# Projection of the node features by rounded high and low parts of weight and features, the weight arriving in two halves

## The chip, the cores and the metric

The kernel runs on one core of a Trainium2 chip. The metric is the device time of one execution in microseconds. The engines are named as the profile names them: PE (TensorE, PEld its weight loads), DVE (VectorE), ACT (ScalarE), POOL (GpSimd) and SP (SyncE, which issues most of the DMA transfers).

## The reference, cut to what matters

Four layers follow one another on 512 node vectors of 768 numbers. The change lies in the first step of the first layer, the projection of the normalised features:

```python
edge_index = jnp.stack([src, dst])                     # 8192 edges, 512 nodes
x = x + _L0_gnn_ref(_layernorm(x), ...)                # three rounds of message passing, attention
x = x + _L0_ffn_ref(_layernorm(x)[None], ...)[0]       # 8 experts, 2 chosen for each node
x = x + _L1_gnn_ref(_layernorm(x), ...)                # two graph attention layers
x = x + _L1_ffn_ref(_layernorm(x)[None], ...)[0]       # 4 experts, 1 chosen

def _L0_gnn_ref(node_features, ...):
    nodes = node_features @ Wn.T + bn                  # 512x768 by 768x768: the step that changes
    edge_proj = edge_features @ We.T + be
    for l in range(3):
        msgs = nodes[src] + nodes[dst] + edge_proj
        agg = jax.ops.segment_sum(msgs, dst, num_segments=n)
        ...
```

## The kernel before, in words

Everything stays in on-chip memory between the layers, and every engine has one program written out by hand in a fixed order; semaphores alone hold them together. There is no planner. `N` is 512 nodes, `NT` = 4 tiles of 128 nodes, `D` = 768, `DC` = 6 blocks of 128 features. Weights arrive in four slots (`slot[0]` to `slot[3]`, 128 x 4608 each), and `part_slot[s]` is the same memory seen as fp32r, the type in which PE takes a rounded fp32 number in one go. PE results go to eight PSUM banks: four (`act_ps`) that ACT empties, four (`dve_ps`) that DVE empties.

The start of the program runs like this.

- SP issues all first loads (L517 to L537): the features `xres` in four tiles, small constants, the weight `wn` into slot 0, indices, two groups of edge features, `we` into slot 1, and the two halves of the first round's weight into slots 2 and 3.
- DVE normalises the features tile by tile (`normalise`, L1762): three tiles together, then the fourth.
- PE turns the normalised tiles around (`turn_features`, L691; 24 transposes, L703) into six banks, one for each block of 128 features.
- ACT and DVE copy three banks each into `xn_t` (L1402, L1811).
- PE multiplies (L740): for each of six output blocks `c`, six matmuls over `k`, each with a 128x128 block of the weight as the kept operand and 128x512 of `xn_t` as the moving one, all in fp32. ACT and DVE take every second result into `nodes_t` with the bias (L1410, L1824).
- PE turns `nodes_t` back into rows (L713), ACT and DVE copy it to `nodes`. ACT has rounded two groups of edge features meanwhile (`ea_hi`, L1406), and DVE forms their remainders (`ea_lo`, L1837).
- Then comes the loop over 64 groups of 128 edges (L758 and L1881), the three rounds, attention, the experts and so on.

Most other products of this kernel are already made in another way, by the helper `mm_parts` (L720): an operand is split into its rounded value (`hi`) and what is left (`lo`), both fp32r, and three matmuls stand for one: hi by hi, hi by lo, lo by hi. In every such place ACT makes the high part by a copy and DVE the low part by a subtraction. The first graph attention layer does this for its features just as the change does it here (L1696 for `xn2_hi`, L2446 for `xn2_lo`).

Of the kernel before, what the change touches and what calls it, by code (L numbers as in the profile page):

```python
# [28 lines left out]
P = 128  # L29
# [7 lines left out]
N = 512  # L37
# [92 lines left out]
def build(nc, x, src, dst, edge, cols, rows, ident_d, iota_d, tri_d, wn, we, w1, w2, wqkv, wo, wg0, e0w1,  # L130
          e0w2, e0b2, gw1, gw2, wg1, e1w1, e1w2, e1b2, xs0, ys0, xs1, ys1, out):
    ctx = ExitStack()
    with ctx:
# [13 lines left out]
        def sem(name):  # L147
            return ctx.enter_context(nc.semaphore(name))
# [53 lines left out]
        def over(name, shape, at, dt=F32):  # L202
            return place(name, shape, dt, area + at)
# [5 lines left out]
        xn_t = over("xn_t", [P, DC, N], 6144)  # L209
# [108 lines left out]
        class Run:  # L318
            def __init__(self, layer, ne, hidden, picks, up, down, scattered, results, b1, b2, up_slots, down_slots, sel_banks, pick_banks):
# [11 lines left out]
                self.filled = sem(f"filled{layer}")  # L331
                self.scattered_in = sem(f"scattered{layer}")
                self.gathered = [sem(f"gathered{layer}_{t}") for t in range(NT)]
                self.sel_set = sem(f"sel_set{layer}")
                self.plan_set = sem(f"plan_set{layer}")
                self.b2_in = sem(f"b2_in{layer}")
                self.last_set = sem(f"last_set{layer}")

        sig0, sig1 = Signals("a"), Signals("b")
# [6 lines left out]
        in_par = sem("in_par")  # L346
        in_ends = sem("in_ends")
# [11 lines left out]
        act_step = sem("act_step")  # L359
# [135 lines left out]
        def _(sp):  # L495
# [27 lines left out]
            load(0, sview(0, DC, D), kview(wn))  # L523
# [59 lines left out]
            def stream_items(run):  # L583

                sp.wait_ge(run.plan_set, 1)
# [40 lines left out]
            def narrow_items(run):  # L626


                sp.wait_ge(run.plan_set, 1)
# [48 lines left out]
        def _(pe):  # L678
# [348 lines left out]
            def rank_tokens(run):  # L1027

                spend(act_ps[3], (14, 6)[run.layer])
                pe.wait_ge(run.sel_set, 1)  # L1030
# [37 lines left out]
            def stream_items(run):  # L1068
# [69 lines left out]
                pe.wait_ge(run.plan_set, 1)  # L1138
# [16 lines left out]
                pe.wait_ge(run.last_set, 1)  # L1155
# [15 lines left out]
            def narrow_items(run):  # L1171
# [52 lines left out]
                pe.wait_ge(run.plan_set, 1)  # L1224
# [13 lines left out]
                pe.wait_ge(run.last_set, 1)  # L1238
# [153 lines left out]
        def _(act):  # L1392
# [199 lines left out]
            def stream_items(run):  # L1592
# [36 lines left out]
                act.wait_ge(run.plan_set, 1)  # L1629
# [9 lines left out]
            def narrow_items(run):  # L1639
# [19 lines left out]
                act.wait_ge(run.plan_set, 1)  # L1659
# [84 lines left out]
        def _(dve):  # L1744
# [458 lines left out]
            def make_plan(run, choices):  # L2203
# [48 lines left out]
                dve.wait_ge(run.plan_set, 1)  # L2252
# [358 lines left out]
            dve.wait_ge(run1.sel_set, 1)  # L2611
# [3 lines left out]
            for t in range(NT):  # L2615
                dve.wait_ge(run1.gathered[t], 16)
# [9 lines left out]
        def _(pool):  # L2626
# [130 lines left out]
```

## Time and profile before

| what | value |
|---|---|
| median of 3 runs | 1350.22 us (1344.23, 1350.22, 1350.96) |
| profiled execution, its own time | 1348.07 us |
| its span, first to last instruction | 1346.5 us |
| PE busy | 95% of the span |
| DVE, ACT, POOL busy | 68%, 43%, 9% |
| mean granted TensorE clock | 0.991 of full speed |

The span is what all rows are counted in; the device time of the same execution lies 1.57 us above it. PE is busy nearly all of the time, but in a fixed order over stages with different limits, so the shares say little of one stage. A PE row named MATMUL shows a modelled end, which overlaps the start of the next one: the pace of a row of matmuls is read from start to start, not from their durations. An fp32 matmul appears as two records (12 for six matmuls).

### The profile page before, as it was taken

To read this page: it belongs to the slowest core of one execution; us is meant where nothing else is said; L and a number is where in the kernel's file an instruction comes from. 1 tells how busy PE (TensorE), PEld (TensorE's weight loads), DVE (VectorE), ACT (ScalarE), POOL (GpSimd) and SP (SyncE) were. 2 spreads that over 40 slices of the span, in tenths; PEclk is the share of its full clock that TensorE was granted. 3 is DMA by queue.
4 is the path that set the end of the run, shared out by engine and by line. 5 is a ranking of instruction groups with operands and counts; after the bars stand their busy time and mean duration, and the time that the engine had idled before them with its cause. 6 is when DMAs were issued, how large, how long until landed. Compare 5 with 4: busy or idle time off the path is not lost. (4 is left out here: it accounts for less than half of the span.)

```text
span 1346.5 us, 19432 instructions
## 1 busy us (share of the span) xinstructions
PE 1280.1 (95%) x7053; PEld 1099.5 (82%) x7054; DVE 911.3 (68%) x1828; ACT 582.8 (43%) x1013; POOL 127.0 (9%) x123
## 2 busy tenths in 40 slices
PE   5999999999999999999999999999999898899997
PEld 2577659969969997666999999999998778796864
DVE  4477683473473465555859999999998778836623
ACT  2011051351350343334418888888986227502110
POOL 0000010000000000003320000000002018600101
PEclk9999999999999999999999999999999998999899
DMA  9321091410410620003158999999998310007134
GB/s 340 136 94 63 9 359 55 153 71 1 153 71 1 235 95 0 1 24 141 67 209 295 356 382 389 390 386 392 389 382 281 137 28 1 1 1 293 47 105 164
DMA packets 80687, 225.46 MB, mean 167 GB/s; under 512 B 5168, under 2 KB 17008, under 8 KB 80496
## 3 DMA queue, kind: packets, MB, share of 16 engines
q1 hardware_dynamic: 72720, 187.64, 37.7%
q0 software_dynamic: 7904, 36.97, 7.6%
q8 instruction: 42, 0.69, 0.2%
q14 instruction: 21, 0.17, 0.0%
HBM read 197.85 MB, written 26.74 MB: 167 GB/s over the span
## 5 line engine op out<-in xcount | busy, mean ns | idle before, releaser
L2116 DVE TENSOR_TENSOR part_slot<-slot,item_hi 128x768 fp32r<-128x768 f32 x150 | 133.5, 958 | 0.2
L1557 ACT ACTIVATE item_hi<-slot 128x768 fp32r<-128x768 f32 x156 | 118.0, 833 | 23.9 <-DMA slot<-in_e0w 19.6
L2125 DVE TENSOR_TENSOR part_slot<-slot,item_hi 128x768 fp32r<-128x768 f32 x132 | 116.6, 954 | 1.7 <-ACT item_hi L1565 1.3
L1565 ACT ACTIVATE item_hi<-slot 128x768 fp32r<-128x768 f32 x132 | 99.1, 831 | 14.6 <-DMA slot<-in_e0w 14.6
L722 PE MATMUL dve_ps<-item_hi,x_hi 128*128 128x384 f32 x288 | 99.3, 345 | 0.5 <-DVE x_lo L2305 0.3
L722 PE MATMUL act_ps<-item_hi,hid_hi 128*128 128x384 f32 x288 | 98.4, 342 | 0.3 <-DVE hid_lo L2317 0.3
L724 PE MATMUL dve_ps<-item_hi,x_lo 128*128 128x384 f32 x288 | 97.2, 338 | 0.0
L723 PE MATMUL act_ps<-part_slot,hid_hi 128*128 128x384 f32 x288 | 96.8, 336 | 0.0
L724 PE MATMUL act_ps<-item_hi,hid_lo 128*128 128x384 f32 x288 | 96.1, 334 | 0.0
L723 PE MATMUL dve_ps<-part_slot,x_hi 128*128 128x384 f32 x288 | 95.6, 332 | 0.0
L1448 ACT ACTIVATE h_t<-act_ps,par 128x256 f32<-128x256 f32 x36 | 21.1, 585 | 121.5 <-PE act_ps L833 121.5
L729 PE MATMUL act_ps<-ones 128*128 128x128 f32 x470 | 62.7, 294 | 8.3 <-DVE gp_t L2520 6.3
L729 PEld LDWEIGHTS act_ps<-ones 128*128 128x128 f32 x470 | 60.3, 208 | 10.9 <-DVE gp_t L2520 6.7
L722 PE MATMUL dve_ps<-h_hi,w_hi 128*128 128x256 f32 x216 | 61.3, 284 | 0.0
L723 PE MATMUL dve_ps<-h_lo,w_hi 128*128 128x256 f32 x216 | 60.7, 281 | 0.0
L724 PE MATMUL dve_ps<-h_hi,part_slot 128*128 128x256 f32 x216 | 60.5, 280 | 0.0
L1967 DVE TENSOR_TENSOR h<-dve_ps,brow 128x384 f32<-128x384 f32 x24 | 13.4, 558 | 63.0 <-PE dve_ps L724 63.0
L722 PEld LDWEIGHTS dve_ps<-item_hi,x_hi 128*128 128x128 f32 x288 | 54.1, 188 | 0.9 <-DVE x_lo L2305 0.5
L722 PEld LDWEIGHTS act_ps<-item_hi,hid_hi 128*128 128x128 f32 x288 | 54.0, 187 | 0.5 <-issue 0.5
L723 PEld LDWEIGHTS dve_ps<-part_slot,x_hi 128*128 128x128 f32 x288 | 54.2, 188 | 0.0
L723 PEld LDWEIGHTS act_ps<-part_slot,hid_hi 128*128 128x128 f32 x288 | 54.2, 188 | 0.0
L724 PEld LDWEIGHTS act_ps<-item_hi,hid_lo 128*128 128x128 f32 x288 | 54.0, 188 | 0.0
(407 smaller groups left out, 3268.9 us busy)
## 6 DMA issues: line engine op xcount, KB each, us to landing
slot<-in_e0w SPq DMA_DIRECT2D x48, 2304.0 KB, 10.4
slot<-in_w SPq DMA_DIRECT2D x9, 2304.0 KB, 9.4
experts<-in_e1w SPq DMA_DIRECT2D x8, 1152.0 KB, 15.3
ea_raw<-in_edge SPq DMA_DIRECT2D x8, 1024.0 KB, 5.5
slot<-in_wqkv SPq DMA_DIRECT2D x3, 2304.0 KB, 14.8
xs<-zrow POOLq DMA_DIRECT2D x2, 3072.0 KB, 15.7
item_x<-xs SPq DMA_DIRECT2D x16, 384.0 KB, 9.6
ys<-item_y POOLq DMA_DIRECT2D x16, 384.0 KB, 6.7
```

Source lines behind the costliest of these rows:

```text
L722: mm(to, kept[0], moved[0], start=start, stop=False)
L723: mm(to, kept[0], moved[1], start=False, stop=False)
L724: return mm(to, kept[1], moved[0], start=False, stop=stop)
L729: mm(bank[:, 0:P], ones[:, :], ones[:, :], start=True, stop=True)
L1448: go(h_t[:, c, ps], turned, ACT.Relu, bias=col("ln_b", at), scale=col("ln_g", at))
L1557: go(item_hi[j][k][:, :], slot[s][:, k * D:(k + 1) * D], ACT.Copy).then_inc(up_high[j], 1)
L1565: go(item_hi[j][k][:, :], slot[s][:, k * D:(k + 1) * D], ACT.Copy).then_inc(down_high[j], 1)
L1967: vv.tensor_tensor(part, bank[:, 0:HALF], brow[:, 0, half * HALF:(half + 1) * HALF], ALU.add).then_inc(sig.dve_freed, 1)
L2116: vv.tensor_tensor(part_slot[s][:, ks], slot[s][:, ks], item_hi[j][k][:, :].bitcast(F32), ALU.subtract).then_inc(up_low[j], 1)
L2125: vv.tensor_tensor(part_slot[s][:, ks], slot[s][:, ks], item_hi[j][k][:, :].bitcast(F32), ALU.subtract).then_inc(down_low[j], 1)
```

## The change

Five things change in the code.

1. `xn_t` goes. In its place stand `xn_hi` and `xn_lo`, both fp32r; `xn_lo` lies where `xres` was, which is dead by then.
2. The weight is split as well: `wn_hi` in six pieces (four in the free part of slot 1, two over `mask`), the low part in place in slot 0, through `part_slot[0]`.
3. ACT makes the six pieces of `wn_hi` and all six of `xn_hi`; DVE makes six low pieces of the weight and all six of `xn_lo`, in the order written.
4. PE uses `mm_parts` for each of the 36 products. For the first output block it waits piece by piece.
5. SP loads `wn` by two transfers (rows 0 to 383 and 384 to 767), the first with a semaphore of its own.

Beside that, some semaphores that the two expert layers had one each of (`filled`, `gathered`, `sel_set`, `plan_set`, `last_set`) are now shared, and each wait on them counts on from the first layer's value.

```diff
-        xn_t = over("xn_t", [P, DC, N], 6144)
+        xn_hi = over("xn_hi", [P, DC, N], 6144, F32R)
+        xn_lo = place("xn_lo", [P, DC, N], F32R, xres_at)
+        wn_hi = [place(f"wn_hi{k}", [P, D], F32R, at) for k, at in
+                 enumerate([4608 + 1536 + D * k for k in range(4)] + [cpt_at, cpt_at + D])]
...
-            load(0, sview(0, DC, D), kview(wn))
+            sp.dma_start(sview(0, DC, D)[:, 0:3, :], kview(wn[0:3 * P, :])).then_inc(in_wn, 16)
+            load(0, sview(0, DC, D)[:, 3:DC, :], kview(wn[3 * P:DC * P, :]))
...
-            pe.wait_ge(slot_in[0], 16)
-            pe.wait_ge(sig.act_freed, ACT0["wn"])
-            pe.wait_ge(sig.dve_freed, DVE0["wn"])
-            wn_s = kslot(0, D)
             for c in range(DC):
-                bank = act_bank(c // 2, ACT0["wn"]) if c % 2 == 0 else dve_bank(c // 2, DVE0["wn"])
+                if c == 0:
+                    bank = act_ps[0]
+                else:
+                    bank = act_bank(c // 2, ACT0["wn"]) if c % 2 == 0 else dve_bank(c // 2, DVE0["wn"])
+                fs = slice(c * P, (c + 1) * P)
                 for k in range(DC):
-                    last = mm(bank[:, :], wn_s[:, k, c * P:(c + 1) * P], xn_t[:, k, :], start=(k == 0), stop=(k == DC - 1))
+                    if c == 0:
+                        pe.wait_ge(wn_low, k + 1)
+                        if k % 2 == 0:
+                            pe.wait_ge(sig.act_freed, ACT0["xt0"] + k // 2 + 1)
+                        else:
+                            pe.wait_ge(sig.dve_freed, DVE0["xt0"] + k // 2 + 1)
+                    last = mm_parts(bank[:, :], (wn_hi[k][:, fs], kslot(0, D, True)[:, k, fs]), (xn_hi[:, k, :], xn_lo[:, k, :]),
+                                    start=(k == 0), stop=(k == DC - 1))
                 last.then_inc(sig.to_act if c % 2 == 0 else sig.to_dve, 1)
...
-            for c in range(0, DC, 2):
-                bank = bank_of(c // 2, ACT0["xt0"])
-                go(xn_t[:, c, :], bank[:, :], ACT.Copy).then_inc(sig.act_freed, 1)
+            for k in range(DC):
+                act.wait_ge(*((in_wn, 16) if k < 3 else (slot_in[0], 16)))
+                go(wn_hi[k][:, :], slot[0][:, k * D:(k + 1) * D], ACT.Copy).then_inc(wn_high, 1)
+            for c in range(DC):
+                if c % 2 == 0:
+                    act.wait_ge(sig.to_act, ACT0["xt0"] + c // 2 + 1)
+                else:
+                    act.wait_ge(sig.to_dve, DVE0["xt0"] + c // 2 + 1)
+                go(xn_hi[:, c, :], (act_ps if c % 2 == 0 else dve_ps)[c // 2][:, :], ACT.Copy).then_inc(xn_high, 1)
...
-            for c in range(1, DC, 2):
-                bank = bank_of(c // 2, DVE0["xt0"])
-                vv.tensor_copy(xn_t[:, c, :], bank[:, :]).then_inc(sig.dve_freed, 1)
+
+            def low_node_weights(k):
+                ks = slice(k * D, (k + 1) * D)
+                dve.wait_ge(wn_high, k + 1)
+                vv.tensor_tensor(part_slot[0][:, ks], slot[0][:, ks], wn_hi[k][:, :].bitcast(F32), ALU.subtract).then_inc(wn_low, 1)
+
+            for k in range(4):
+                low_node_weights(k)
+            for c in range(DC):
+                bank, freed = ((act_ps[c // 2], sig.act_freed), (dve_ps[c // 2], sig.dve_freed))[c % 2]
+                dve.wait_ge(xn_high, c + 1)
+                vv.tensor_tensor(xn_lo[:, c, :], bank[:, :], xn_hi[:, c, :].bitcast(F32), ALU.subtract).then_inc(freed, 1)
+                if c in (1, 3):
+                    low_node_weights(4 + c // 2)
...
-                pool.wait_ge(run.filled, 64)
+                pool.wait_ge(run.filled, 128)
                 pool.wait_ge(normed, normed_by)
-                pool.wait_ge(run.plan_set, 1)
+                pool.wait_ge(run.plan_set, run.layer + 1)
```

On DVE, this stood between the end of the normalisation (`xn`) and the first result of the projection (`nodes_t`) before:

```order
35 L1798 TENSOR_SCALAR xn<-xres,mv,rstd 128x768
36 L1811 COPY xn_t<-dve_ps 128x512 x3
37 L1813 CAST ends<-ends_i 128x128
38 L1815 TENSOR_SCALAR src_w<-ends 128x64
39 L1817 SCALAR_TENSOR_TENSOR src_at<-src_w,ends 128x64
40 L1819 TENSOR_SCALAR src_w<-src_w 128x64
41 L1820 TENSOR_SCALAR zero<-iota 128x512
42 L1824 TENSOR_SCALAR nodes_t<-dve_ps,par 128x512 x3
```

And now (`slot_49` is slot 0, `part_slot_54` the same memory as fp32r, `wn_hi_108` to `wn_hi_113` the six pieces):

```order
35 L1820 TENSOR_SCALAR xn<-xres,mv,rstd 128x768
36 L1835 TENSOR_TENSOR part_slot_54<-slot_49,wn_hi_108 128x768
37 L1835 TENSOR_TENSOR part_slot_54<-slot_49,wn_hi_109 128x768
38 L1835 TENSOR_TENSOR part_slot_54<-slot_49,wn_hi_110 128x768
39 L1835 TENSOR_TENSOR part_slot_54<-slot_49,wn_hi_111 128x768
40 L1842 TENSOR_TENSOR xn_lo<-act_ps,xn_hi 128x512
41 L1842 TENSOR_TENSOR xn_lo<-dve_ps,xn_hi 128x512
42 L1835 TENSOR_TENSOR part_slot_54<-slot_49,wn_hi_112 128x768
43 L1842 TENSOR_TENSOR xn_lo<-act_ps,xn_hi 128x512
44 L1842 TENSOR_TENSOR xn_lo<-dve_ps,xn_hi 128x512
45 L1835 TENSOR_TENSOR part_slot_54<-slot_49,wn_hi_113 128x768
46 L1842 TENSOR_TENSOR xn_lo<-act_ps,xn_hi 128x512
```

Three copies became twelve subtractions; the index work (`ends` to `zero`) moved behind them.

On PE, behind the last transpose of the features, stood six fp32 matmuls for each output block:

```order
26 L740 MATMUL act_ps<-xn_t,slot_49 128x512 [waits dve_freed_a,act_freed_a,slot_in0]
27 L740 MATMUL act_ps<-xn_t,slot_49 128x512 x5
28 L740 MATMUL dve_ps<-xn_t,slot_49 128x512 [waits dve_freed_a]
29 L740 MATMUL dve_ps<-xn_t,slot_49 128x512 x5
30 L740 MATMUL act_ps<-xn_t,slot_49 128x512 [waits act_freed_a]
```

Now there are eighteen, and the first block waits at each `k`:

```order
26 L731 MATMUL act_ps<-xn_hi,wn_hi_108 128x512 [waits act_freed_a,wn_low]
27 L732 MATMUL act_ps<-xn_lo,wn_hi_108 128x512
28 L733 MATMUL act_ps<-xn_hi,part_slot_54 128x512
29 L731 MATMUL act_ps<-xn_hi,wn_hi_109 128x512 [waits dve_freed_a,wn_low]
30 L732 MATMUL act_ps<-xn_lo,wn_hi_109 128x512
31 L733 MATMUL act_ps<-xn_hi,part_slot_54 128x512
```

One wait at the head of the projection became six, each for a low piece of the weight and a low piece of the features.

## Rows read from the trace of the kernel before

**Rows 1.** The page: span and busy time of each engine.

```profile
span 1346.5 us, 19432 instructions
PE 1280.1 (95%) x7053; PEld 1099.5 (82%) x7054; DVE 911.3 (68%) x1828; ACT 582.8 (43%) x1013; POOL 127.0 (9%) x123
```

**Rows 2.** Timeline of the start: start us, us, engine, line, operation, count, [idle before].

```profile
4.96 0.44 SPq L498 DMA_DIRECT2D slot<-in_wn  x1
...
13.69 0.45 PE L703 MATMUL act_ps<-ident,xn 128*128 128x128 f32 x1 [13.69 <-DVE xn L1798]
...
17.06 0.68 DVE L1798 TENSOR_SCALAR xn<-xres,mv,rstd 128x768 f32<-128x768 f32 x1
...
18.40 0.27 PE L703 MATMUL dve_ps<-ident,xn 128*128 128x128 f32 x1
...
20.42 7.09 PE L740 MATMUL act_ps<-xn_t,slot 128*128 128x512 f32 x12 [1.75 <-DVE xn_t L1811]
...
20.63 1.91 ACT L1406 ACTIVATE ea_hi<-ea_raw 128x2048 fp32r<-128x2048 f32 x1 [0.90 <-DMA ea_raw<-in_edge]
...
27.34 5.31 PE L740 MATMUL dve_ps<-xn_t,slot 128*128 128x512 f32 x12
```

**Rows 3.** Timeline from the end of the projection to the edge loop.

```profile
51.80 1.45 PE L740 MATMUL dve_ps<-xn_t,slot 128*128 128x512 f32 x3
53.29 0.75 DVE L1824 TENSOR_SCALAR nodes_t<-dve_ps,par 128x512 f32<-128x512 f32 x1 [9.55 <-PE dve_ps L740]
...
57.47 2.35 DVE L1837 TENSOR_TENSOR ea_lo<-ea_raw,ea_hi 128x1024 fp32r<-128x1024 f32 x2
57.65 1.16 PE L753 MATMUL act_ps<-zero 128*128 128x512 f32 x4 [0.70 <-ACT nodes L1413]
```

**Rows 4.** Transfers: size, median us from issue to landing.

```profile
slot<-in_e0w SPq DMA_DIRECT2D x48, 2304.0 KB, 10.4
...
slot<-in_wn SPq DMA_DIRECT2D x1, 2304.0 KB, 11.7
```

**Rows 5.** Stretches of the start: busy time, then PEclk, DMA share, GB/s.

```profile
0.00:10.00 10.00, 0.00 (x0) 0.01 (x1) 4.53 (x17) 1.30 (x2) 0.22 (x5) 1.00 0.72 229
10.00:16.00 6.00, 2.31 (x11) 2.35 (x12) 5.40 (x23) 0.00 (x0) 0.00 (x0) 1.00 1.03 398
18.70:20.40 1.70, 0.00 (x0) 0.01 (x1) 1.67 (x5) 1.04 (x3) 0.00 (x0) 1.00 1.09 349
20.40:23.40 3.00, 2.98 (x4) 1.45 (x5) 0.88 (x4) 1.91 (x1) 0.00 (x0) 0.51 1.07 375
24.40:25.40 1.00, 1.00 (x4) 0.51 (x3) 0.00 (x0) 1.00 (x1) 0.00 (x0) 1.00 1.06 412
```

**Rows 6.** Timeline at 480 us: one weight split by ACT and DVE.

```profile
482.71 4.50 ACT L1500 ACTIVATE wv_hi<-slot 128x768 fp32r<-128x768 f32 x6
483.95 5.30 DVE L2022 TENSOR_TENSOR part_slot<-slot,wv_hi 128x768 fp32r<-128x768 f32 x6
```

**Rows 7.** Timeline at 1063 us: features split out of PSUM, first parts multiplied.

```profile
1063.14 0.60 ACT L1696 ACTIVATE xn_hi<-act_ps 128x512 fp32r<-128x512 f32 x1 [12.28 <-PE act_ps L703]
...
1063.77 0.69 DVE L2446 TENSOR_TENSOR xn_lo<-act_ps,xn_hi 128x512 fp32r<-128x512 f32 x1 [2.49 <-ACT xn_hi L1696]
...
1064.61 0.47 PE L722 MATMUL act_ps<-gw_hi,xn_hi 128*128 128x512 f32 x1 [0.96 <-DVE xn_lo L2446]
...
1065.55 0.65 ACT L1696 ACTIVATE xn_hi<-dve_ps 128x512 fp32r<-128x512 f32 x1
...
1066.77 0.68 DVE L2446 TENSOR_TENSOR xn_lo<-dve_ps,xn_hi 128x512 fp32r<-128x512 f32 x1
```

**Rows 8.** Timeline at 1092 us: parts multiplied in a steady row.

```profile
1092.01 0.39 PE L723 MATMUL act_ps<-part_slot,xn_hi 128*128 128x512 f32 x1
...
1097.80 0.40 PE L724 MATMUL dve_ps<-gw_hi,xn_lo 128*128 128x512 f32 x1
```

**Rows 9.** Stretches at 480 us: PE in groups of three behind DVE.

```profile
485.00:489.40 4.40, 4.03 (x16) 2.46 (x16) 4.40 (x6) 4.40 (x8) 0.00 (x0) 1.00 0.45 129
```

**Rows 10.** Waits, 56 to 690 us, the longest two: who, total us, times, longest.

```profile
POOL part_slot L2681 <- ACT part_slot L1525: 447.0, 2, 441.7
POOL xs L2635 <- PE dve_ps L795: 164.8, 1, 164.8
```

**Rows 11.** Waits on DMA, 690 to 1346 us, on the expert weights.

```profile
ACT item_hi L1557 <- DMA slot<-in_e0w: 19.6, 19, 1.9
ACT item_hi L1565 <- DMA slot<-in_e0w: 14.6, 10, 2.3
```

**Rows 12.** The stretch of the first expert layer.

```profile
690.00:1060.00 370.00, 362.93 (x2204) 355.76 (x2204) 343.09 (x490) 287.44 (x501) 28.47 (x38) 1.00 0.93 350
```

More of the change, by code:

```diff
@@ L330, in __init__ @@
                 self.y_out = sem(f"y_out{layer}")
-                self.filled = sem(f"filled{layer}")
+                self.filled = filled
                 self.scattered_in = sem(f"scattered{layer}")
-                self.gathered = [sem(f"gathered{layer}_{t}") for t in range(NT)]
-                self.sel_set = sem(f"sel_set{layer}")
-                self.plan_set = sem(f"plan_set{layer}")
+                self.gathered = gathered
+                self.sel_set = sel_set
+                self.plan_set = plan_set
                 self.b2_in = sem(f"b2_in{layer}")
-                self.last_set = sem(f"last_set{layer}")
+                self.last_set = last_set
+        filled, sel_set, plan_set, last_set = sem("filled"), sem("sel_set"), sem("plan_set"), sem("last_set")
+        gathered = [sem(f"gathered{t}") for t in range(NT)]
         sig0, sig1 = Signals("a"), Signals("b")
@@ L346, in build @@
         in_par = sem("in_par")
+        in_wn = sem("in_wn")
+        wn_high = sem("wn_high")
+        wn_low = sem("wn_low")
+        xn_high = sem("xn_high")
         in_ends = sem("in_ends")
@@ L358, in build @@
         dve_step = sem("dve_step")
-        act_step = sem("act_step")
         normed = sem("normed")
@@ L583, in stream_items @@
             def stream_items(run):
-                sp.wait_ge(run.plan_set, 1)
+                sp.wait_ge(run.plan_set, run.layer + 1)
                 last = sp.value_load(plan_i[0:1, 16:17], min_val=run.items_min - 1, max_val=run.items_max - 1)
@@ L626, in narrow_items @@
             def narrow_items(run):
-                sp.wait_ge(run.plan_set, 1)
+                sp.wait_ge(run.plan_set, run.layer + 1)
                 last = sp.value_load(plan_i[0:1, 16:17], min_val=run.items_min - 1, max_val=run.items_max - 1)
@@ L1029, in rank_tokens @@
                 spend(act_ps[3], (14, 6)[run.layer])
-                pe.wait_ge(run.sel_set, 1)
+                pe.wait_ge(run.sel_set, run.layer + 1)
                 ne = run.ne
@@ L1137, in stream_items @@
                 turn_x(1)
-                pe.wait_ge(run.plan_set, 1)
+                pe.wait_ge(run.plan_set, run.layer + 1)
                 last = pe.value_load(plan_i[0:1, 16:17], min_val=run.items_min - 1, max_val=run.items_max - 1)
@@ L1153, in stream_items @@
                 turn_hidden(last)
-                pe.wait_ge(run.last_set, 1)
+                pe.wait_ge(run.last_set, run.layer + 1)
                 for t in range(NT):
@@ L1223, in narrow_items @@
                 turn_row(1)
-                pe.wait_ge(run.plan_set, 1)
+                pe.wait_ge(run.plan_set, run.layer + 1)
                 last = pe.value_load(plan_i[0:1, 16:17], min_val=run.items_min - 1, max_val=run.items_max - 1)
@@ L1236, in narrow_items @@
                 turn_wide(last)
-                pe.wait_ge(run.last_set, 1)
+                pe.wait_ge(run.last_set, run.layer + 1)
                 pe.wait_ge(turned_kept, 2 * (last + 2))
@@ L1628, in stream_items @@
                 x_in(1)
-                act.wait_ge(run.plan_set, 1)
+                act.wait_ge(run.plan_set, run.layer + 1)
                 last = act.value_load(plan_i[0:1, 16:17], min_val=run.items_min - 1, max_val=run.items_max - 1)
@@ L1658, in narrow_items @@
                 x_in(1)
-                act.wait_ge(run.plan_set, 1)
+                act.wait_ge(run.plan_set, run.layer + 1)
                 last = act.value_load(plan_i[0:1, 16:17], min_val=run.items_min - 1, max_val=run.items_max - 1)
@@ L2251, in make_plan @@
                 vv.tensor_copy(plan_i[:, :], plan[:, :]).then_inc(run.plan_set, 1)
-                dve.wait_ge(run.plan_set, 1)
+                dve.wait_ge(run.plan_set, run.layer + 1)
             def second_rows(run, n):
@@ L2610, in _ @@
             vv.tensor_copy(sel[:, 0:NT, 0:NE1], pick[0][:, :, 0:NE1]).then_inc(run1.sel_set, 1)
-            dve.wait_ge(run1.sel_set, 1)
+            dve.wait_ge(run1.sel_set, 2)
             make_plan(run1, (pick[0],))
@@ L2615, in _ @@
             for t in range(NT):
-                dve.wait_ge(run1.gathered[t], 16)
+                dve.wait_ge(run1.gathered[t], 48)
                 then(vv.tensor_tensor(xres[:, t, :], xres[:, t, :], got[:, t, 0, :], ALU.add))
```

## The prediction

> **What bounds the kernel now.** I read the page first: PE is busy for 95% of the span [rows 1], in one fixed order, so any time taken from PE's row in the projection should come off the end unless something behind it runs by a clock of its own. Then the timeline of the first 60 us. The reader is to see one chain: DVE ends the normalisation at 17.74 (17.06 + 0.68), PE turns the last tile until 18.7, ACT and DVE copy, and PE starts the projection at 20.42 and is never idle in it until its end [rows 2, 3]. The last result is taken at 53.29. The projection thus costs 53.25 - 20.42 = 32.8 us, all of it on the path. What comes behind it (taking `nodes_t`, turning it, `ea_lo` at 57.47) hangs on its end alone: ACT and DVE stand waiting for PE there, 9.55 us in the row shown [rows 3].
>
> The pace inside: 12 records of one block take 32.49 - 27.34 = 5.15 us (5.31 with the drain of the last one), so one fp32 matmul costs 0.858 us, a quarter of that is 0.215 [rows 2]. Third view, the clock: PE was granted 1.00 until its pause of 1.75 us, 0.51 (the 1.2 GHz level) from 20.40 to 23.40, and 1.00 (2.4 GHz) from 24.40 on [rows 5]. So some 3.5 us were run at half speed.
>
> **What goes.** 36 fp32 matmuls of 0.858 us are 30.9 us, and 1.9 us more went by the low clock. Three copies on ACT and three on DVE go too.
>
> **What comes on PE.** 108 fp32r matmuls 128x512. Their pace in a row without waits: from 1092.01 to 1097.80 stand 25 steps, 5.79 / 25 = 0.2316 us [rows 8]. 36 products then cost 36 x 3 x 0.2316 = 25.0 us against 30.9: 5.9 us less. From below the pace is bounded by the fp32 quarter, 0.215 [rows 2]; I take 0.2316, because it is the same shape, type and helper. The Trainium skill (FP8 and Floating Point Precision, section TensorE Precision Notes) says that true fp32 takes four passes through the array. By it alone three parts would cost 3/4, and the saving would be 7.7 us and not 5.9; the trace has 0.858 / 0.2316 = 3.7 and decides the sum, and the other figure is a rival below.
>
> **What comes before PE can start.** This is the price of the change.
> - Landing. `wn` was issued at 4.96 and landed 11.7 us later, at 16.7 [rows 2, 4]. The queues were full and moved 229, then 398 GB/s [rows 5], so the first half (1.18 MB, some 3 us of traffic) lands at about 13.6, an estimate from these rows; the second at 16.7.
> - ACT. A high piece of the weight comes every 0.75 us (4.50 / 6) and takes 0.83 [rows 6]. Pieces 0 to 2: 13.6 to 15.9. Pieces 3 to 5: 16.7 to 19.0. Then `xn_hi` every 0.48 us ((1065.55 - 1063.14) / 5) [rows 7]: the first from 19.0 to 19.6, the last ends at 22.1. The two edge groups behind it start at 22 instead of 20.63, last 1.9 us each, and are not wanted before 57.47 less the gain [rows 2, 3]: 30 us of cover, no cost.
> - DVE. It is busy until 17.74 anyway. A low piece of the weight comes every 0.87 us ((5.30 - 0.95) / 5) [rows 6], a low piece of the features every 0.60 ((1066.77 - 1063.77) / 5) and ends 0.68 after its start [rows 7]. Four weight pieces: 17.74 to 21.2; their high parts are there (the fourth at 17.5). `xn_lo` 0 starts at 21.2, ends at 21.9; then 1, weight 4, `xn_lo` 2, 3, weight 5, `xn_lo` 4 and 5, with starts at 21.8, 22.4, 23.3, 23.9, 24.5, 25.4 and 26.0. The last ends at 26.7. DVE sets the start, not ACT and not the transfer.
> - PE. 0.15 us lie between the end of the first `xn_lo` and the first matmul [rows 7], so it starts at 22.05, after a pause of 3.4 us. It will be at 1.2 GHz again, as after the pause of 1.75 us. I take the same 3.5 us of it. A part then costs 0.43: k = 0 and 1 until 24.6, two thirds of k = 2 until 25.5, the rest at full speed, and k = 2 to 5 end at 25.7, 26.4, 27.1, 27.8. DVE alone would allow 26.8 + 0.7 = 27.5, so both limits nearly meet and the low clock costs 0.3 here, where it cost 1.9 before.
>
> **The sum.** First block done at 27.8. Five blocks follow: 90 x 0.2316 = 20.8, the last matmul starting at 48.4 and ending 0.39 later, at 48.75. Against 53.25 that is **4.5 us less**. Put otherwise: 5.9 from the matmuls and 1.9 - 0.3 = 1.6 from the low clock, less some 3 us for the later start and the steps in which PE waits for DVE.
>
> Bounds: the start. If the weight landed as late as the next transfer, whose landing let ACT start at 20.63 [rows 2], the first `xn_lo` would come at 24.2 and the first block end near 29.1: 3.2 us gained. If PE kept the full clock: 27.5, 4.8 gained. With the lower bound of the pace as well, 90 x 0.0166 = 1.5 more: 6.3 gained. Splitting the transfer is worth under 0.7 us: with both halves at 16.7 ACT would end its weight at 21.3 and the first `xn_lo` at 22.6.
>
> **Edits at nothing.** One more DMA issue on SP, 0.44 us [rows 2], ahead of transfers that sit in full queues. DVE's index work ends near 28 instead of 21.35, first wanted by PE at 57.65 [rows 3]; its cover is 25 us. The shared semaphores: POOL now waits for all eight fills before the first experts; they are issued from 164.8 us on in one go [rows 10], and the experts begin at 690. The other waits only count higher.
>
> **Is the gain handed on?** Between 56 and 690 us the list of waits is led by engines waiting for engines [rows 10], and none of its lines names a DMA as the releaser, so the transfers of the rounds follow the engines' signals and have slack. In the expert layer ACT waits for the weight stream, 19.6 + 14.6 us [rows 11], but its first loads are themselves released by PE's progress and move along. Nothing found runs by its own time, so I pass on the whole gain.
>
> Against the profiled execution: 1348.07 - 4.5 = 1343.6 us. The runs of before lie from 1344.23 to 1350.96, which is more than the gain; the profiled one is 2.2 below their median, and the mean of all four is 1348.4. I take the predicted time from that mean: **1344.0**. What a measurement of this kernel can tell from no change is about 0.5%, here 6.7 us.
>
> **The rivals.**
> - *Parts at the fp32 pace* (gain 6 us, 1342.4). The 0.2316 of rows 8 would have to come from that stage and not from the operand type. For it: fp32 shows 0.215 in the same banks. Against it: the row of the same helper. Chance 0.08.
> - *Late start* (gain 2 to 3.5 us, 1345.5). The weight lands later or ACT is late, by the bound above. For it: the queues are full from 10 to 25 us. Chance 0.12.
> - *Nothing is left at the end* (1348.4). A stage behind absorbs it, the expert stream being the candidate whose DMA share is 0.93 [rows 12]. Against it: its first load is released by PE. Chance 0.10.
> - *Slower: the clock does not come back.* In the first block PE works in groups of three behind DVE. If that left it at 1.2 GHz for the whole projection, 108 x 0.43 = 46.4 us would end at 68.5, 15 us later than before: 1363. The point from which it decides: each part at the low level costs 0.2 us extra, so 4.5 / 0.2 = 23 more of them, 10 us, i.e. a rise after 35 instead of 25.5. Against it: at 485 us PE works in just such groups and the clock stays at 1.00 [rows 9], but there it was high to begin with. For it: one pause of 1.75 us was enough to lose it [rows 5]. Chance 0.04. The Trainium skill (TensorE: Matmul & The Clock Gate, section HAM oscillation) describes bursts shorter than the waits between them, which restart at the low clock each time; here the waits (up to 0.9 us) are shorter than three parts at the low clock (1.3 us), so the trace's sums leave PE no gap.
> - *The change moves the routing*: a rounding that alters the number of expert items costs or saves a whole item, some 30 us (370 us of expert layer for 48 / 4 = 12 items) [rows 4, 12]. Chance 0.01.
>
> The forecast has 0.65. Two executions of one kernel differ by up to 6.7 us, so part of each case falls on the other side of the bound: **faster** by over 0.5% 0.33 (two fifths of the forecast, over half of the first rival), **within** 0.60, **slower** 0.07 (the clock, routing, a disturbed median in the absorbed case). The range is 1338.5 (best bound, less the scatter) to 1350.5 (nothing gained, with the scatter).
>
> **What would show it.** In the changed kernel's timeline: the first part matmul near 22.0, the last near 48.4, `nodes_t` taken at about 48.8 instead of 53.29, pace 0.23 in the last five blocks, granted clock 0.5 until about 25.5, DVE without a wait from 17.06 to 26.7. All later stages should start 4.5 us earlier. I am wrong if DVE waits for ACT's high pieces, if the parts run at another pace, if the clock stays low beyond 30 us, or if the stages behind do not move with the projection.

## The result, and the profile after

The changed kernel ran in 1343.91 us (median of 20 runs, 1339.95 to 1347.84), the kernel before in 1347.40 us (20 runs, 1343.21 to 1350.96). The ratio is 0.9975, 95% interval 0.9965 to 0.9985: 3.4 us faster, between 2.0 and 4.7. Forecast were 4.5 us, 1344.0 us, and "within 0.5%" as the likeliest verdict. The verdict holds. That the time agrees to 0.1 us is luck: the forecast subtracted a gain about 1 us too large from a starting time 1 us too high (1348.4, where the 20 runs have 1347.40). Two more comparisons below gave 0.9983 and 0.9987. Weighted by their intervals the three give 2.7 us (about 1.7 to 3.7, an estimate), so the 4.5 us hold for the first comparison alone.

The page of the changed kernel, to set beside [rows 1]:

```profile
span 1341.8 us, 19527 instructions
PE 1276.1 (95%) x7089; PEld 1107.3 (83%) x7090; DVE 918.2 (68%) x1837; ACT 589.3 (44%) x1022; POOL 127.7 (10%) x123
```

PE is 4.0 us less busy, while DVE and ACT took on 6.9 and 6.5 us.

From here on stretches of a profile are compared by one distance: from DVE's end of the normalisation (`xn`) to the start of its last take of `nodes_t`. It was 53.29 - 17.74 = 35.55 us before [rows 2, 3]. It leaves out how early the features happened to arrive, which differs from execution to execution (DVE was done at 17.74 before and at 16.43 + 0.68 = 17.11 after).

The timeline of the changed kernel's start, where ACT, DVE and PE split and multiply (start us, us, engine, line, operation, [idle before]):

```profile
13.02 2.31 ACT L1418 ACTIVATE wn_hi<-slot 128x768 fp32r<-128x768 f32 x3 [10.71 <-DMA slot<-in_wn]
...
16.18 2.31 ACT L1418 ACTIVATE wn_hi<-slot 128x768 fp32r<-128x768 f32 x3 [0.85 <-DMA slot<-in_wn]
...
16.43 0.68 DVE L1820 TENSOR_SCALAR xn<-xres,mv,rstd 128x768 f32<-128x768 f32 x1
...
17.03 3.56 DVE L1835 TENSOR_TENSOR part_slot<-slot,wn_hi 128x768 fp32r<-128x768 f32 x4
...
18.40 0.57 ACT L1424 ACTIVATE xn_hi<-act_ps 128x512 fp32r<-128x512 f32 x1
...
20.50 0.68 DVE L1842 TENSOR_TENSOR xn_lo<-act_ps,xn_hi 128x512 fp32r<-128x512 f32 x1
...
21.33 0.47 PE L731 MATMUL act_ps<-xn_hi,wn_hi 128*128 128x512 f32 x1 [2.62 <-DVE xn_lo L1842]
...
27.39 0.40 PE L731 MATMUL dve_ps<-xn_hi,wn_hi 128*128 128x512 f32 x1
```

The first `xn_hi` was ready at 18.97, the first `xn_lo` began at 20.50: DVE was still at its four low weights. The second block starts at 27.39. At the end of the projection:

```profile
47.92 0.40 PE L733 MATMUL dve_ps<-xn_hi,part_slot 128*128 128x512 f32 x1
48.35 0.75 DVE L1857 TENSOR_SCALAR nodes_t<-dve_ps,par 128x512 f32<-128x512 f32 x1 [7.55 <-PE dve_ps L733]
```

The last five blocks take 89 steps from 27.39 to 47.92, 0.2307 us each. The last take starts at 48.35, against 53.29 before; the distance is 31.24, 4.3 us less. The clock, in stretches (the figure behind the five engines is PEclk):

```profile
20.00:21.30 1.30, 0.00 (x0) 0.00 (x1) 1.30 (x3) 1.30 (x4) 0.00 (x0) 1.00 1.09 348
21.30:22.40 1.10, 1.07 (x5) 0.93 (x6) 1.10 (x2) 1.10 (x2) 0.00 (x0) 1.00 1.10 371
22.40:25.80 3.40, 3.26 (x9) 2.08 (x8) 3.40 (x6) 2.73 (x2) 0.00 (x0) 0.51 1.03 400
25.90:26.90 1.00, 1.00 (x5) 0.81 (x5) 0.90 (x6) 0.00 (x0) 0.00 (x0) 1.00 1.04 406
```

The low clock (0.5, the 1.2 GHz level) came, but 1.1 us after PE had started again, and lasted 3.4 us. In two other executions of the same kernel it was there from the first part matmul on, at 20.81 and 20.76, and lasted for 5.4 us of the products; the distance was 31.89 in both. In the third profile:

```profile
20.80:24.00 3.20, 3.20 (x8) 2.55 (x9) 3.20 (x5) 3.10 (x4) 0.00 (x0) 0.50 1.07 378
24.00:26.00 2.00, 2.00 (x6) 1.55 (x5) 1.90 (x7) 1.71 (x1) 0.00 (x0) 0.50 1.04 404
```

Is the shift handed on? Here is one group of each later stage, by tile, with its first and last start; the last row names the last expert layer:

```profile
L1486 ACT ACTIVATE nt_hi<-nodes_t x18: 612/613/629, 168.0 to 378.0; 128x512 fp32r<-128x512 f32 x18
...
L1519 ACT ACTIVATE na_hi<-nodes_t x6: 614/614/630, 474.7 to 477.3; 128x512 fp32r<-128x512 f32 x6
...
L1673 ACT ACTIVATE hid_t<-act_ps,par x18: 360/368/370, 1278.6 to 1323.0; 128x128 f32<-128x128 f32 x18
```

The same of the kernel before:

```profile
L1464 ACT ACTIVATE nt_hi<-nodes_t x18: 612/613/629, 172.9 to 382.9; 128x512 fp32r<-128x512 f32 x18
...
L1497 ACT ACTIVATE na_hi<-nodes_t x6: 613/616/630, 479.6 to 482.2; 128x512 fp32r<-128x512 f32 x6
...
L1651 ACT ACTIVATE hid_t<-act_ps,par x18: 359/367/369, 1283.4 to 1327.8; 128x128 f32<-128x128 f32 x18
```

The shift is 4.9 us at each point up to attention and 4.8 in the last layer; the spans are 1346.5 and 1341.8. Of it 4.3 us are the distance and 0.6 the earlier features. In this pair of profiles nothing absorbs it.

### The profile page after: what moved, and what is told of

The parts are those of the page before. It is cut to its first block and busy times, and to the rows that moved or that the text cites. A ratio compares the mean times of both kernels' runs of the same rounds, so it can differ in the third digit from the quotient of the medians.

```text
span 1341.8 us, 19527 instructions
## 1 busy us (share of the span) xinstructions
PE 1276.1 (95%) x7089; PEld 1107.3 (83%) x7090; DVE 918.2 (68%) x1837; ACT 589.3 (44%) x1022; POOL 127.7 (10%) x123
## 5 line engine op out<-in xcount | busy, mean ns | idle before, releaser
L2000 DVE TENSOR_TENSOR h<-dve_ps,brow 128x384 f32<-128x384 f32 x24 | 13.4, 556 | 63.1 <-PE dve_ps L733 63.1
```

## The experiments

All ratios are against runs of the kernel before on the same chip, 29 or 35 of them to 12 of the experiment (6 with two parts, 5 with the later end; 20 to 20 in the first comparison of the changed kernel). Where a ratio is turned into microseconds below, it is the ratio times the median of before; the difference of two medians can lie a microsecond or two beside it. Each distance and tail is that of one execution. "Tail" is the rest of the span behind the last take of `nodes_t`.

| kernel | distance | first part matmul after `xn` | tail | ratio (95% interval) |
|---|---|---|---|---|
| before | 35.55 | | 1293.2 | |
| shared semaphores only | 35.56 | | 1289.6 | 1.0006 (0.9994 to 1.0017) |
| before, pause filled | 34.35 | | 1290.0 | 0.9999 (0.9985 to 1.0012) |
| before, 10.1 us added behind | 35.40 | | 1303.3 | 1.0109 (1.0092 to 1.0125) |
| changed | 31.24 | 4.22 | 1293.5 | 0.9975 (0.9965 to 0.9985) |
| changed, again | 31.89 | 4.22 | 1293.1 | 0.9983 (0.9968 to 0.9998) |
| changed, third | 31.89 | 4.22 | 1289.7 | 0.9987 (0.9973 to 1.0002) |
| one transfer | 32.33 | 5.26 | 1296.5 | 1.0010 (0.9996 to 1.0024) |
| one transfer, again | 33.10 | 5.40 | 1297.0 | 1.0000 (0.9986 to 1.0014) |
| DVE order | 30.64 | 2.48 | 1293.2 | 0.9992 (0.9980 to 1.0005) |
| order and two blocks | 28.46 | 3.26 | 1296.2 | 0.9981 (0.9966 to 0.9996) |
| order and two blocks, again | 29.23 | 2.48 | 1295.7 | 0.9981 (0.9967 to 0.9996) |
| early start, two blocks | 28.21 | 2.60 | 1296.2 | 0.9981 (0.9965 to 0.9996) |
| two parts | 23.89 | 4.23 | 1290.6 | 0.9934 (0.9917 to 0.9951) |

**The shared semaphores alone.**

```diff
-                self.filled = sem(f"filled{layer}")
+                self.filled = filled
...
-                pool.wait_ge(run.filled, 64)
+                pool.wait_ge(run.filled, 128)
```

Expected: 

> The kernel before with the shared semaphores alone. The distance meant here and below is the one from DVE's end of the normalisation to the start of its last take of nodes_t: 35.55 us before, 31.24 after. Theory (sharing costs nothing): distance 35.5, ratio to before 1.000. Rival (the shared waits release earlier or later and carry part of the difference): same distance, but a ratio off by 0.001 or more and a later stage at another offset.

Distance 35.56, ratio 1.0006 with 1 inside its interval. Sharing costs nothing that can be measured: the projection has not moved, and the interval leaves room for 0.8 us less to 2.3 us more.

**One transfer.**

```diff
-            sp.dma_start(sview(0, DC, D)[:, 0:3, :], kview(wn[0:3 * P, :])).then_inc(in_wn, 16)
-            load(0, sview(0, DC, D)[:, 3:DC, :], kview(wn[3 * P:DC * P, :]))
+            load(0, sview(0, DC, D), kview(wn))
...
-                act.wait_ge(*((in_wn, 16) if k < 3 else (slot_in[0], 16)))
+                act.wait_ge(slot_in[0], 16)
```

Expected: 

> The changed kernel with the weight in one transfer. Theory (DVE sets the start, halves are worth little): all six high weights from about 16.2 to 20.9, first low weight at about 17.1, first low part of the features about 0.5 to 1.0 us later than 20.50, the distance 31.7 to 32.2, ratio to before 0.9975 to 0.998. Rival (the first half's early landing carries the gain): the distance grows by over 2 us and the ratio goes to 0.999 or more.

The timeline of its start:

```profile
16.13 4.51 ACT L1417 ACTIVATE wn_hi<-slot 128x768 fp32r<-128x768 f32 x6 [13.83 <-DMA slot<-in_wn]
...
17.01 3.57 DVE L1834 TENSOR_TENSOR part_slot<-slot,wn_hi 128x768 fp32r<-128x768 f32 x4 [0.28 <-ACT wn_hi L1417]
...
21.15 0.69 DVE L1841 TENSOR_TENSOR xn_lo<-act_ps,xn_hi 128x512 fp32r<-128x512 f32 x1 [0.58 <-ACT xn_hi L1423]
```

Now ACT sets the start: `xn_hi` comes behind six high weights, and DVE waits for it. The distance grew by 1.1 us, a little over the forecast of 0.5 to 1.0. But the ratio is not the 0.998 that the distance gives; it was 1.0010, outside what theory said and on the rival's side, and this was run again.

Expected of the repeat: 

> One transfer of the weight once more; the first time its distance was as forecast (32.3 us) and its ratio was not (1.001). Theory (the ratio was the scatter of clock dips behind the projection): ratio 0.9975 to 0.999 here, about 1 us above the changed kernel. Rival (something behind the projection regularly costs it 3 us, as the dip of the clock near 165 us in its profile): ratio 1.000 to 1.001 again, and the granted clock at 160 to 200 us below 1.00 again.

Distance 33.10, ratio 1.0000. The rival's figure came true, its place did not: the clock at 160 to 200 us was low in the first profile and not in the second, where instead the expert layer took 3.6 us longer than in the changed kernel (358.8 us from the first `xn_hi` to the last `hid_t` against 355.2). DVE's first low part of the features begins 4.4 and 4.6 us behind `xn` in the two profiles, against 3.4 in the changed kernel: 1.0 to 1.2 us later. The distances differ by 0.4 to 1.9 us, according to which profiles are compared, since the low clock lies elsewhere in each; against the two of the changed kernel in which it was low from the first product on, by 0.4 to 1.2. In device time it is 1.8 to 4.7 us between its ratios and those of the changed kernel; why more is open.

**Two parts.** The product of high weight and low features is left out.

```diff
-                    last = mm_parts(bank[:, :], (wn_hi[k][:, fs], kslot(0, D, True)[:, k, fs]), (xn_hi[:, k, :], xn_lo[:, k, :]),
+                    mm(bank[:, :], wn_hi[k][:, fs], xn_hi[:, k, :], start=(k == 0), stop=False)
+                    last = mm(bank[:, :], kslot(0, D, True)[:, k, fs], xn_hi[:, k, :], start=False, stop=(k == DC - 1))
```

Expected: 

> The changed kernel without the product of high weight and low features (36 of 108 part matmuls left out of the projection, so the result lacks that part). Theory (each part costs its pace, 0.23 us, and the whole is handed on to the end): five blocks lose 30 x 0.23 = 7 us, the first block, which waits for DVE, loses 0.5 to 1; distance about 23.5, ratio to before 0.992 (10.8 to 12 us under before). Rival (something behind absorbs part of any gain): distance about 23.5 too, but the ratio stays above 0.994.

DVE's takes of `nodes_t` in its timeline:

```profile
28.90 0.75 DVE L1857 TENSOR_SCALAR nodes_t<-dve_ps,par 128x512 f32<-128x512 f32 x1 [2.89 <-PE dve_ps L756]
34.37 0.75 DVE L1857 TENSOR_SCALAR nodes_t<-dve_ps,par 128x512 f32<-128x512 f32 x1 [4.72 <-PE dve_ps L756]
39.91 0.75 DVE L1857 TENSOR_SCALAR nodes_t<-dve_ps,par 128x512 f32<-128x512 f32 x1 [4.79 <-PE dve_ps L756]
```

Two blocks take 39.91 - 34.37 = 5.54 us, 24 parts of 0.231: each part costs its pace, whatever its place in the triple. Distance 23.89, as expected. The ratio gives 8.9 us less (6.6 to 11.2) where the distance gives 11.7: short again, between theory (0.992) and rival (above 0.994). Inside its profile the gain is handed on. The rows of the three later stages:

```profile
L1486 ACT ACTIVATE nt_hi<-nodes_t x18: 612/613/629, 159.5 to 369.5; 128x512 fp32r<-128x512 f32 x18
...
L1519 ACT ACTIVATE na_hi<-nodes_t x6: 613/616/630, 466.2 to 468.8; 128x512 fp32r<-128x512 f32 x6
...
L1673 ACT ACTIVATE hid_t<-act_ps,par x18: 359/367/369, 1267.4 to 1311.8; 128x128 f32<-128x128 f32 x18
```

Against before, `nt_hi` and `na_hi` are 13.4 us earlier: 11.7 of the distance and 1.7 of earlier features. The last layer is 16.0 earlier, because here it had no dip of the clock ahead of it and before had one (see below). A gain of 11.7 us meets no stage that keeps it.

**The pause of the kernel before, filled.**

```diff
             turn_features(xn, ACT0["xt0"], DVE0["xt0"], 0)
+            pe.wait_ge(const_set, 2)
+            spend(act_ps[3], 7)
```

Expected: 

> The kernel before with seven idle fp32 matmuls 128x128 of ones on a free bank between the last transpose and the projection, so that PE has no pause there. Theory (of the 32.8 us of the old projection 1.9 were lost to the low clock after the pause): granted clock 1.00 from the pause on, the distance 33.7 to 34.2, ratio 0.9985. Rival (the low clock comes whatever PE does there): a stretch at 0.5 stays, distance 35.5 or more.

Two stretches of this kernel around the former pause:

```profile
17.60:20.00 2.40, 2.40 (x19) 2.40 (x18) 2.33 (x6) 1.25 (x3) 0.00 (x0) 1.00 1.09 348
20.00:23.40 3.40, 3.40 (x11) 1.49 (x10) 0.53 (x2) 1.93 (x2) 0.00 (x0) 1.00 1.08 372
```

No low clock follows in this profile. The distance fell by 1.2 us, less than the 1.4 to 1.9 foreseen: PE started 3.25 us behind `xn` instead of 2.68. The stretch from its first product to the last take is 1.8 us shorter, which is the price of the low clock. The ratio does not resolve it.

That the filling kept the clock up is not shown by it. In this profile the last transposes ran at the low level still, 0.21 us apart:

```profile
17.67 0.42 PE L703 MATMUL act_ps<-ident,xn 128*128 128x128 f32 x1
17.88 0.42 PE L703 MATMUL dve_ps<-ident,xn 128*128 128x128 f32 x1
```

In five profiles it was so, and the clock rose only after them. In four of these it then stayed up, with the pause filled (here and in the early start below) and with the pause left as it is (DVE's other order, and the first profile of two blocks); in the fifth, the changed kernel's first, it fell 1.1 us into the products. In the nine others the last transposes ran at the high level, and the clock was low with the first product or within 0.3 us of it. So filled and unfilled pauses don't differ here once that is taken into account, and the mean granted clock of the 12 timed executions, 0.9907 against 0.9905 (standard error 0.0006), doesn't show it either: 3.4 us less of the low clock in each would be 0.0013 more.

**The changed kernel again.** Expected the second time: 

> The changed kernel once more, beside the next three on one chip. Theory (the projection is 4.3 us shorter and the whole is handed on, executions scatter by some 4 us): distance from DVE's end of the normalisation to the last take of nodes_t 31.2, ratio to before 0.9965 to 0.998. Rival (part of the gain is eaten behind the projection): same distance, ratio 0.999 or more.

Expected the third time: 

> The changed kernel a third time, beside these on one chip. Theory: distance 31.2 to 31.9 as in its two profiles (the clock falls at another moment in each), ratio 0.997 to 0.998, so that the three comparisons together give 3 to 4 us. Rival (the gain is not real beyond the first comparison): ratio 0.999 or more.

Distances 31.89 and 31.89, 3.7 us under before (the first repeat had 31.2 as its forecast); ratios 0.9983 and 0.9987, both between what theory and rival said. The third interval reaches 1.0002. By the ratios the changed kernel is 3.4, 2.3 and 1.8 us under before, by the medians 3.5, 2.1 and 3.0.

**DVE in another order.**

```diff
-            for k in range(4):
+            for k in range(2):
                 low_node_weights(k)
             for c in range(DC):
+                if c >= 2:
+                    low_node_weights(c)
```

Expected: 

> The changed kernel with DVE's low parts in another order: two low weights, then features and weights in turn, so that the first low part of the features is ready when ACT has made its high part. Theory (DVE's four low weights hold PE back, but the end of the first block is set by DVE's last low part, which stays where it was): first part matmul at about 19.9 instead of 21.3, first block's end about 0.6 us earlier (the low clock is then hidden in DVE's pace), distance 30.6. Rival (PE's start alone counts): distance 29.8, 1.4 us less.

Its timeline at the start of the projection:

```profile
19.03 0.68 DVE L1844 TENSOR_TENSOR xn_lo<-act_ps,xn_hi 128x512 fp32r<-128x512 f32 x1
19.63 0.68 DVE L1844 TENSOR_TENSOR xn_lo<-dve_ps,xn_hi 128x512 fp32r<-128x512 f32 x1
...
19.86 0.47 PE L731 MATMUL act_ps<-xn_hi,wn_hi 128*128 128x512 f32 x1 [0.88 <-DVE xn_lo L1844]
...
21.92 0.47 PE L731 MATMUL act_ps<-xn_hi,wn_hi 128*128 128x512 f32 x1 [0.40 <-DVE xn_lo L1844]
```

PE starts 2.48 us behind `xn` instead of 4.22, then waits for each low part. The distance is 30.64: 0.6 less than the shorter of the changed kernel's, and not 1.4. This looks like theory, but the granted clock was 1.00 from the first product on in this profile, where theory had it low. The last products of the first block, here and in the third profile of the changed kernel:

```profile
26.32 0.47 PE L731 MATMUL act_ps<-xn_hi,wn_hi 128*128 128x512 f32 x1 [0.54 <-DVE xn_lo L1844]
```

```profile
26.77 0.39 PE L731 MATMUL act_ps<-xn_hi,wn_hi 128*128 128x512 f32 x1
```

DVE's last low part ends 8.80 us behind `xn` in both orders. Here PE waits for it and starts its last three parts at 8.94; in the changed kernel PE comes to them without a wait, at 9.58 and, with the longer low clock, at 10.23 and 10.25. So DVE's twelve subtractions as a whole set the earliest end of the first block, and an earlier start alone is worth little; and what the changed kernel lies above that end is the low clock, 0.6 or 1.3 us of it. What the order itself is worth this run can't tell.

**The first two blocks made together**, on top of that order, k outermost, in the two banks without turned features.

```diff
+            for k in range(DC):
+                pe.wait_ge(wn_low, k + 1)
...
+                for c, bank in enumerate((act_ps[3], dve_ps[3])):
+                    project(c, k, bank)
```

Expected: 

> That order, and the first two output blocks made together, k outermost, in the two banks that hold no turned features. Theory (PE now has 1.39 us of work for each 1.47 us of DVE, so DVE's pace no longer costs anything and the start is worth its full 1.4 us): both blocks done at about 29.9 with 3.5 us of low clock, 28.2 without, against 31.5 in the changed kernel; distance 29.6 with the low clock, 27.9 without; ratio to before 0.9955 to 0.997. Rival (the low clock takes what the order gives): distance 31.

Distance 28.46, ratio 0.9981, short of the 0.9955 to 0.997 expected. The clock was at 1.00 here, for which 27.9 was given: PE started 3.26 us behind `xn` and not 2.48, because ACT was still at its high weights when the first features were turned (its first `xn_hi` began at 1.81). It was run again. Expected: 

> The kernel with DVE's other order and two blocks together once more. Its distance was 28.5 us, 7.1 under before, its ratio only 0.9981, with dips of the clock near 165 us and before the last expert layer in its profile. Theory (such dips come by chance): distance 28 to 29 again, ratio 0.995 to 0.997. Rival (they belong to this kernel): ratio 0.998 again and the stretch from the first nt_hi to the first na_hi 308 us again instead of 306.7.

Distance 29.23, with the low clock this time (29.6 was given for that), ratio 0.9981, and the stretch from the first `nt_hi` to the first `na_hi` was 308.4 us in both, where the changed kernel has 306.6 to 306.7. The rival holds on both counts. The stretch where it arises, in the first of the two:

```profile
162.00:164.00 2.00, 0.03 (x1) 0.00 (x0) 2.00 (x4) 1.94 (x3) 2.00 (x3) 1.00 1.01 357
164.00:166.00 2.00, 1.65 (x4) 0.96 (x5) 0.45 (x2) 2.00 (x4) 1.13 (x2) 0.94 1.00 355
166.00:168.00 2.00, 2.00 (x3) 0.69 (x3) 2.00 (x4) 2.00 (x5) 0.00 (x0) 0.50 1.01 358
168.00:170.00 2.00, 2.00 (x5) 0.77 (x4) 2.00 (x4) 2.00 (x4) 0.00 (x0) 0.71 1.02 358
```

And the same place of the changed kernel:

```profile
165.00:167.00 2.00, 0.00 (x0) 0.00 (x0) 2.00 (x4) 1.98 (x3) 2.00 (x3) 1.00 0.98 346
167.00:169.00 2.00, 1.69 (x4) 0.87 (x5) 0.45 (x2) 2.00 (x4) 1.10 (x2) 1.00 0.99 353
169.00:171.00 2.00, 2.00 (x6) 0.94 (x5) 2.00 (x4) 2.00 (x5) 0.00 (x0) 1.00 1.02 360
```

Both have the same pause of 2.3 us of PE. Behind it one falls to 1.2 GHz and loses 1.7 us, the other doesn't.

**Early start.** Two blocks, one low weight ahead, ACT's last two high weights moved between its high features, three fillers in the pause.

```diff
+            spend(act_ps[3], 3)
...
+            for k in range(4):
+                high_node_weights(k)
             for c in range(DC):
+                if c in (2, 4):
+                    high_node_weights(3 + c // 2)
```

Expected: 

> The kernel with two blocks together, and with only one low weight ahead of the first low features on DVE, with ACT making the last two high weights between its high features, and with three idle matmuls in PE's pause. Theory (start and low clock are the two prices of the split): first part matmul near 19.5, no stretch at half clock, both first blocks done near 28.1, distance 27 to 28, ratio to before 0.9935 to 0.996. Rival (the starts no longer matter, PE waits for DVE's low parts all along): distance 28.5 to 29.5.

PE started at 19.02, the clock stayed at 1.00, and the first two blocks were taken at 27.39 and 28.10. The forecast of 28.1 is met by luck: the features came 0.7 us early (`xn` at 16.42), and counted from them the blocks came 0.7 late. So the distance of 28.21 lies over the range, between theory and rival, and the ratio 0.9981 is outside what was expected. The dip at 165 us was there as well (308.4).

**A later end, for the handing on.** 50 fillers between the projection and the turning of its result.

```diff
                 last.then_inc(sig.to_act if c % 2 == 0 else sig.to_dve, 1)
+            spend(act_ps[3], 50)
```

Expected: 

> The kernel before with 50 idle fp32 matmuls 128x128 (about 12 us) put between the end of the projection and the turning of its result. In the runs so far the timed ratios stayed 1 to 4 us short of what the distances in the profiles gave. Theory (what happens to the projection's end is handed on in full, the shortfall is scatter behind it and at the start): time up by what the profile shows for the fillers, 11 to 13 us, ratio 1.0085 to 1.0095. Rival (a stage behind absorbs a share of any shift, a quarter as in the run with two parts): up by 9 us or less, ratio 1.0065 or less.

The timeline of this kernel at the fillers:

```profile
51.93 0.75 DVE L1825 TENSOR_SCALAR nodes_t<-dve_ps,par 128x512 f32<-128x512 f32 x1 [9.55 <-PE dve_ps L740]
62.89 0.49 PE L713 MATMUL act_ps<-ident,nodes_t 128*128 128x128 f32 x3
```

From the take to the turning lie 10.96 us, where 54.15 - 53.29 = 0.86 lay before: 10.1 added (the forecast of 11 to 13 was off). The ratio gives 14.7 us (12.4 to 16.7; the medians differ by 13.0). A stage that absorbed a share of each shift would have given under 10: the rival is refuted for a delay. A gain is another matter, since a stage that waits for something with a time of its own can pass a delay on and still keep a gain. For that the run with two parts is the test: its 13.4 us at `nt_hi` and `na_hi` are all there.

## Why the prediction was right, and where it was off

**What goes and what comes on PE** was right. Parts at 0.2307 us against 0.2316 forecast; the rival of 0.215 would have ended the five last blocks 1.4 us earlier. The run with two parts has the same pace. True fp32 takes four passes through the array by the Trainium skill (FP8 and Floating Point Precision, section TensorE Precision Notes); as an estimate, taken as a ratio of times, that would give this rival's pace. The trace has 0.858 / 0.2307 = 3.7 and decides.

**The start** was right: 22.05 - 17.74 = 4.3 us behind `xn` forecast, 4.22 measured in three profiles, with DVE's four low weights as the cause: with two ahead of it, it was 2.48. DVE's last low part was forecast to end 26.7 - 17.74 = 9.0 us behind `xn` and ended at 8.8. The halves landed where they should, 13.0 and 16.2 against 13.6 and 16.7.

**The low clock** was sized too small, and its moment varies. I took 3.5 us of it from PE's first part matmul on, at a price of 0.3 us, because DVE's limit lay nearly as late. In the two profiles in which it did begin there it lasted for 5.4 us of the products; in the one above it came 1.1 us later. With the clock at 1.00 the second block began 9.71 us behind `xn` (DVE in another order), where the forecast for that case was 27.5 - 17.74 = 9.76. With the low clock it was 10.27, 10.92 and 10.95: a price of 0.6 or 1.2 us and not 0.3. The distance of 31.24 beside the forecast of 48.8 - 17.74 = 31.1 therefore agrees in part by luck; it is 31.89 where the clock did what the sum assumes. What makes it fall here is not shown: the level at which the last transposes ran sorts 13 of the 14 profiles, and the filled pause doesn't settle it.

**The worth of the halves** was given as under 0.7 us. DVE's first and last low parts of the features came 1.0 to 1.2 us later without them, and the distances leave 0.4 to 1.2 us where the clock was low from the start: the term was too small rather than wrong in kind.

**The handing on** was right in its mechanism: no stage absorbs, as the stage-by-stage shifts of 4.9 us and, with two parts, of 13.4 us show. But the time on the wall does not follow the distances to better than some microseconds. Every altered kernel came out slower than its distance says, by 0.8 to 4.8 us: the changed one by 0.9, 1.4 and 1.9, the late end by 4.6, the two blocks by 3.8 to 4.8. Part of it is seen in the profiles: the tail is 1289.6 to 1293.2 in the kernel before and its close kin (1293.2 with the 10.1 us taken off), and 1289.7 to 1297.0 in the others. Its steps are dips of the clock behind pauses that every kernel has, 1.7 us near 165 us, and 2.7 us ahead of the last expert layer (15.2 to 16.0 us from the last `xn_hi` to its first matmul in ten profiles, the first of before among them, and 13.3 in four), besides the expert stream (353.9 to 358.8). The dip at 165 us stood in three of three profiles of the kernels with two blocks, in one of two with one transfer, and in none of the other nine. I had called the routes behind the projection free of clocks of their own; that step failed for TensorE's clock.

That it is not chance alone, the timed executions show, for each has its mean granted clock on record. The 93 of the kernel before average 0.9901, the 44 of the changed kernel 0.9887, the 24 with one transfer 0.9877, the 36 with two blocks 0.9882 (standard errors 0.0002 to 0.0004). Within every kernel the slower executions are those with the lower clock (the correlation of time and clock over all, each kernel taken by itself, is -0.80), and where PE sets the pace 0.001 less of it is worth 1.3 us of 1345. Taking off what the low clock inside the projection costs, which is already in the distances, the rest comes to 3.0 to 4.1 us for the kernels with two blocks, whose shortfall is 3.8 to 4.8, and to about two thirds of the shortfalls of all twelve comparisons behind the first together. These are estimates: they take each kernel's one profile for the projections of all its executions. For the changed kernel it comes to nothing in the second comparison and 0.9 us in the third, so its missing 0.9 to 1.9 us stay open in the main, as does the reason why the altered kernels are granted less clock.

Among the rivals, the late start, the fp32 pace, the absorption and the lasting low clock did not occur. Two further versions beat the kernel before, by 0.19% in each of three comparisons; neither is shown to beat the changed kernel, though their projections are 2 to 3.7 us shorter.

## What to carry to other kernels

Replacing fp32 matmuls by three fp32r parts saves about a fifth of their time here (0.858 to 3 x 0.231 us), and the splitting is paid at the head: count the vector operations that must be done before the first block can end, not before it can begin. Spread such operations so that the matrix engine has other blocks to do meanwhile: that shortened the projection here by 2 to 3.7 us, though the measured time doesn't show it. A gain of a few microseconds in a program of 1.3 ms is read better as a distance inside the profile than as a time, because each pause of the matrix engine may or may not cost a stretch at half clock. The distance moves with that clock too, by 0.6 to 0.8 us here between profiles of one kernel, so look at the granted clock of both stretches before comparing them, and at the mean clock of every timed run. To test whether a gain is handed on, make a larger gain; a stage can pass a delay on that would keep a gain.

## What the runs showed of the hardware that was not expected

- The clock column can miss a low clock at the start. From 12 to 17 us it reads 1.00 in the changed kernel, while 128x128 transposes start 0.21 us apart; the same ones are 0.11 apart in the kernel before from 17.1 us on:

```profile
16.70 0.42 PE L703 MATMUL act_ps<-ident,xn 128*128 128x128 f32 x1
16.91 0.35 PE L703 MATMUL dve_ps<-ident,xn 128*128 128x128 f32 x1
17.10 0.27 PE L703 MATMUL act_ps<-ident,xn 128*128 128x128 f32 x1
17.21 0.27 PE L703 MATMUL dve_ps<-ident,xn 128*128 128x128 f32 x1
```

  PE had done nothing but these transposes before the spacing changed at 16.9 us. In the changed kernel's first profile all 24 ran at the low level, and the rise came between the last of them (18.29) and the second part matmul (21.64), while PE paused for the most part. Where no change of the clock has been recorded yet, the spacing tells its level and the column doesn't.
- The clock fell while PE was busy (1.1 us into the first block), and after the same pause it fell in some executions and not in others.
- The arrival of the first features varied by 1.8 us between profiles (`xn` done at 16.02 to 17.81).
